# Moving a second gate, a residual and a scaled copy between the engines of a fused Mamba and FFN kernel

## The reference, cut to what matters

```
xbc  = silu(causal conv of 4 taps of the projection)          # X, B, C
Y_intra = (C B^T * decay * dt) X                              # within a chunk
Y_inter = (C H_prev) * exp(cum)      per token and head       # from the chunks before
y = (Y_intra + Y_inter + D_skip * X) * silu(z)                # the gate
out = rmsnorm(y) @ out_proj.T
x = x + layernorm(u + out)                                    # the residual
...
w = silu((h . down_embed) * softmax(top-8 scores))            # per head, 4 heads
x = x + layernorm(w @ up_embed + dense FFN)
```

## Time and profile before

| | |
|---|---|
| median of 3 runs | 2841.09 us (2840.73 to 2841.52) |
| the profiled execution, its own time | 2840.37 us |
| its span, first to last instruction | 2838.7 us |
| mean granted TensorE clock | 0.972 |
| PE busy | 2684.0 us (95%) |
| VectorE busy | 2449.3 us (86%) |
| GpSimd busy | 2100.9 us (74%) |
| ScalarE busy | 1737.2 us (61%) |

### The profile page before, as it was taken

One profiled execution on the slowest core, in us unless ns is written; L12 is line 12 of the kernel. 1 busy time (PEld: TensorE's weight loads), 2 busy tenths in 40 slices (PEclk: granted clock), 3 DMA queues, 4 the chain that ended last, 5 costly groups with the idle time before them and its releaser, 6 DMA issues. The chain is left out here.

```text
span 2838.7 us, 50280 instructions
## 1 busy us (share of the span) xinstructions
PE 2684.0 (95%) x14720; PEld 2215.7 (78%) x14720; DVE 2449.3 (86%) x6310; ACT 1737.2 (61%) x3656; POOL 2100.9 (74%) x2689
## 2 busy tenths in 40 slices
PE   5899999999999999999999999999999999999985
PEld 4778887878887878887878887878887878887864
DVE  4588898998888998889898889988889988989985
ACT  4566666666666566666666666666666666666643
POOL 3377777877777877777877777877777877777866
PEclk9999999999999999999999999999999999999998
DMA  3000000000000000000000000000000000000000
GB/s 133 8 8 12 5 7 11 11 11 11 4 7 11 11 11 11 4 7 11 11 11 11 4 7 11 11 11 11 4 7 11 11 11 8 7 7 11 8 5 8
DMA packets 28182, 34.23 MB, mean 12 GB/s; under 512 B 2672, under 2 KB 27248, under 8 KB 27440
## 3 DMA queue, kind: packets, MB, share of 16 engines
q1 hardware_dynamic: 28144, 33.77, 3.8%
HBM read 25.37 MB, written 8.39 MB: 12 GB/s over the span
## 5 line engine op out<-in xcount | busy, mean ns | idle before, releaser
L1079 DVE SCALAR_TENSOR_TENSOR acc<-bank,cw,acc 128x253 f32<-128x253 f32 (+2 forms) x1920 | 773.5, 470 | 0.0
L1405 PE MATMUL bank<-hT,w_in 128*128 128x256 f32 x2560 | 606.3, 382 | 11.4 <-DVE acc L1079 10.8
L594 POOL TENSOR_TENSOR Em<-ee 128x1024 f32<-128x1024 f32 x256 | 578.8, 2280 | 11.3 <-issue 11.3
L1405 PEld LDWEIGHTS bank<-hT,w_in 128*128 128x128 f32 x2560 | 485.0, 192 | 118.2 <-issue 44.5
L1238 DVE SCALAR_TENSOR_TENSOR Em<-Em,p 128x1024 f32<-128x1024 f32 x256 | 407.1, 1590 | 0.0
L609 POOL TENSOR_TENSOR W<-W,Em 128x1024 f32<-128x1024 f32 x128 | 337.0, 2633 | 8.5 <-ACT Em L887 0.3
L755 ACT ACTIVATE acc<-bank,cb,cw 128x256 f32<-128x256 f32 x640 | 325.1, 561 | 0.0
L1247 DVE TENSOR_TENSOR Em<-Em,products 128x1024 f32<-128x1024 f32 x256 | 310.9, 1214 | 4.5
L887 ACT ACTIVATE Em<-Em,rden 128x1024 f32<-128x1024 f32 x256 | 292.0, 1142 | 33.9 <-DVE Em L1247 33.9
L1574 PE MATMUL products<-w_de,h2T 128*128 128x512 f32 x512 | 234.5, 601 | 17.7 <-DVE Em L1247 17.7
L736 ACT ACTIVATE xbcT<-acc 128x512 f32<-128x512 f32 x320 | 200.6, 627 | 74.1 <-DVE acc L1079 74.0
(11 more groups left out here) (196 smaller groups left out, 5578.9 us busy)
## 6 DMA issues: line engine op xcount, KB each, us to landing
x_in<-x_dram SPq DMA_DIRECT2D x32, 256.0 KB, 2.7
x_res<-x_dram SPq DMA_DIRECT2D x32, 256.0 KB, 2.7
out_dram<-f SPq DMA_DIRECT2D x32, 256.0 KB, 2.2
w_in<-in_wT_dram SPq DMA_DIRECT2D x1, 3080.0 KB, 12.0
w_up<-upT_dram SPq DMA_DIRECT2D x1, 1024.0 KB, 14.7
w_de<-down_eT_dram SPq DMA_DIRECT2D x1, 1024.0 KB, 16.7
w_down<-downT_dram SPq DMA_DIRECT2D x1, 1024.0 KB, 18.7
w_ue<-up_e_dram SPq DMA_DIRECT2D x1, 1024.0 KB, 20.8
```

The source lines that it names most:

```text
L594: nc.gpsimd.tensor_tensor(Em[:, k], bc(ee[:, k, 0:XD], 2, KEYS), bc(ee[:, k, XD:XD + KEYS], 1, XD), ALU.mult).then_inc(E_done.sem, 1)
L1079: ins = V.scalar_tensor_tensor(acc[:, r, a, ahead:], ps[:, a * TOK:(a + 1) * TOK - ahead], cw[:, t, k:k + 1], acc[:, r, a, ahead:], ALU.mu ...
L1405: last = mm(ring[j % 2][:, a * TOK:(a + 1) * TOK], w_in[:, k, at:at + P], hT[:, k, :], start=k == 0, stop=k == DK - 1)
```

## The change

Five edits, all in the order and placement of work; what is computed stays the same.

1. `mixer_state` goes from VectorE to ScalarE. One VectorE multiply of 512 columns becomes eight ScalarE instructions of 64 columns, each with its head's `ecum` as the per-partition scale. It stands after `mixer_B(g, 0)` for c = 0, and after the first expert head for c = 1. ScalarE's `ffn_norm(f)` moves two steps later, behind `mixer_square(g, 1)`.
2. VectorE's `mixer_gate(g, 1)` and `mixer_step(g, 1)` go ahead of `ffn_mask(e, 0, 2)`. On GpSimd, `weigh(e, 1, 0)` now waits for `y_done(g, 1)`, and `mixer_decay(g, 1)` goes ahead of `ffn_root(f)`.
3. `tail_residual(e)` goes ahead of both convolutions 0 and 1. On GpSimd, `tail_root4` follows `tail_root3` at the end of the turn and no longer stands at the start of the next; both stand ahead of `collect(e, 0, 1)` and behind one head of `weigh`.
4. `ffn_last` no longer multiplies by the root and the last product (L1229, twice a group); the reciprocal is multiplied in once for both chunks in `ffn_choose`, and the last product becomes the scale of ScalarE's silu.
5. The matmul of zeros in `ffn_down` goes; the first matmul of the group starts the bank.

```diff
+                if gate is not None:
+                    pool.wait_ge(y_done.sem, y_done.at(gate, CH - 1))
                 for h in heads:
...
                 if a:
                     mixer_dt_abs(g)
-                if b:
-                    tail_root4(e)
...
                     mixer_scale(g, 1)
+                    mixer_decay(g, 1)
                 if c:
                     ffn_root(f)
-                if a:
-                    mixer_decay(g, 1)
-                if b:
-                    weigh(e, 1, 0, 1)
+                if b:
+                    weigh(e, 1, 0, gate=g)
                 if a:
                     mixer_root_y(g)
                 if b:
+                    weigh(e, 1, 1)
+                if a:
+                    tail_root3(g)
+                    tail_root4(g)
+                if b:
                     collect(e, 0, 1)
-                if a:
-                    tail_root3(g)
-                if b:
                     weigh(e, 1, 2, 3)
...
+            def mixer_state(g, c):
+
+                act.wait_ge(Yi_ps.sem, Yi_ps.at(g, c))
+                act.wait_ge(ecum_done.sem, ecum_done.at(g))
+
+                if later(g):
+                    act.wait_ge(yT_ps.sem, yT_ps.at(g - 1, c))
+                    act.wait_ge(sq_done.sem, sq_done.at(g - 1, c))
+                for h in range(HEADS):
+                    last = nc.scalar.activation(yv[:, c, h * HD:(h + 1) * HD], ring[1 - c][:, h * HD:(h + 1) * HD],
+                                                ACT.Identity, scale=ecum[:, 0, c, h:h + 1])
+                last.then_inc(Yi_read.sem, 1)
...
-                    nc.scalar.activation(cls[:], clz[:, c], ACT.Silu, accum_out=clsum[:, c:c + 1])\
+                    nc.scalar.activation(cls[:], clz[:, c], ACT.Silu, scale=last_a[:, 0:1],
+                                         accum_out=clsum[:, c:c + 1])\
...
                     mixer_B(g, 0)
+                    mixer_state(g, 0)
                 if n is not None:
                     mixer_hT(n)
...
                     ffn_experts(e, 0, 0)
                 if a:
+                    mixer_state(g, 1)
                     mixer_yT(g, 0)
-                if c:
-                    ffn_norm(f)
                 if b:
                     ffn_experts(e, 0, 1)
                 if a:
                     mixer_yT(g, 1)
                     mixer_square(g, 1)
+                if c:
+                    ffn_norm(f)
...
+                V.tensor_tensor(masked, masked, bc(rden[:].rearrange("p c h -> p (c h)"), 2, NC), ALU.mult)\
+                    .then_inc(clz_done.sem, 1)
...
-                V.scalar_tensor_tensor(clz[:, c], clz[:, c], last_a[:, 0:1], bc(rden[:, c], 2, NC),
-                                       ALU.mult, ALU.mult).then_inc(clz_done.sem, 1)
+                V.tensor_copy(last_a[:], fA[:, EXPERTS - 1:]).then_inc(last_done.sem, 1)
...
-                conv(0)
                 if b:
                     tail_residual(e)
-                conv(1)
+                conv(0, 1)
...
                 if a:
-                    mixer_state(g, 0)
                     mixer_scores(g, 0)
...
                 if b:
                     ffn_mask(e, 0, 1)
-                if a:
-                    mixer_state(g, 1)
                 if b:
                     ffn_times(e, 0, 1)
-                    ffn_mask(e, 0, 2)
                 if a:
                     mixer_gate(g, 1)
                     mixer_step(g, 1)
                 if b:
+                    ffn_mask(e, 0, 2)
                     ffn_times(e, 0, 2)
...
-                    mm(f0[:], zero_b[:], mask_b[:].rearrange("p h t -> p (h t)"), start=True, stop=False)
                 for i in range(FT):
                     last = mm(f0[:, c * D:(c + 1) * D], hid[:, i, c * P:(c + 1) * P], w_down[:, i, :],
-                              start=False, stop=False)
+                              start=c == 0 and i == 0, stop=False)
```

More of the change, by code:

```diff
@@ L123, in sandwich @@
         ident_b = sb("ident_b", [P, P], BF16)
-        zero_b = sb("zero_b", [P, P], BF16)
         mask_b = sb("mask_b", [P, 4, P], BF16)
@@ L270, in sandwich @@
         Z_done = sig("Z_done", CH * RH)
-        clz_done, cls_done = sig("clz_done", CH), sig("cls_done", CH)
+        clz_done, last_done, cls_done = sig("clz_done"), sig("last_done", CH), sig("cls_done", CH)
         W_part, W_done = sig("W_part", CH * (RH - 1)), sig("W_done", CH)
@@ L341, in _ @@
             nc.gpsimd.memset(mask_b[:], 0.0).then_inc(own_pool, own.one())
-            nc.gpsimd.memset(zero_b[:], 0.0).then_inc(own_pool, own.one())
             nc.gpsimd.memset(halo[:], 0.0).then_inc(own_pool, own.one())
@@ L582, in tail_root4, with weigh @@
                 nc.gpsimd.tensor_tensor(shift4[:], rs4[:], neg_mean4[:], ALU.mult).then_inc(root4.sem, 1)
-            def weigh(e, c, *heads):
+            def weigh(e, c, *heads, gate=None):
+                if gate is not None:
+                    pool.wait_ge(y_done.sem, y_done.at(gate, CH - 1))
                 for h in heads:
@@ L654, in do_group @@
                 if b:
-                    collect(e, 0, 1)
+                    weigh(e, 1, 1)
                 if a:
                     tail_root3(g)
+                    tail_root4(g)
                 if b:
+                    collect(e, 0, 1)
                     weigh(e, 1, 2, 3)
@@ L875, in ffn_experts @@
                 if 0 in heads:
-                    act.wait_ge(clz_done.sem, clz_done.at(e, c))
+                    act.wait_ge(clz_done.sem, clz_done.at(e))
+                    act.wait_ge(last_done.sem, last_done.at(e, c))
                     if c or later(e):
@@ L1096, in mixer_scores @@
                                     Ldec[:, 4 * q:4 * q + 4, :], ALU.mult).then_inc(sL_done.sem, 1)
[L1098 to L1106, removed]
             def mixer_step(g, c):
@@ L1221, in ffn_choose @@
                 V.reciprocal(rden[:].rearrange("p c h -> p (c h)"), den[:]).then_inc(rden_done.sem, 1)
+                dve.wait_ge(rden_done.sem, rden_done.at(e))
+                dve.wait_ge(own_dve, own.n)
+                V.tensor_tensor(masked, masked, bc(rden[:].rearrange("p c h -> p (c h)"), 2, NC), ALU.mult)\
+                    .then_inc(clz_done.sem, 1)
             def ffn_last(e, c):
                 dve.wait_ge(A_ps.sem, A_ps.at(e, c))
-                dve.wait_ge(rden_done.sem, rden_done.at(e))
-                V.tensor_copy(last_a[:], fA[:, EXPERTS - 1:]).then_inc(own_dve, own.one())
-                dve.wait_ge(own_dve, own.n)
-                V.scalar_tensor_tensor(clz[:, c], clz[:, c], last_a[:, 0:1], bc(rden[:, c], 2, NC),
-                                       ALU.mult, ALU.mult).then_inc(clz_done.sem, 1)
+                if c or later(e):
+                    dve.wait_ge(cls_done.sem, cls_done.at(e, c - 1))
+                V.tensor_copy(last_a[:], fA[:, EXPERTS - 1:]).then_inc(last_done.sem, 1)
             def ffn_mask(e, c, *heads):
```

## The result

| | before | after |
|---|---|---|
| median of 4 runs, us | 2841.31 | 2936.72 (2935.62 to 2939.07) |
| ratio | | 1.0337 [1.0319, 1.0355] |
| profiled execution: time, span | 2840.37, 2838.7 | 2936.50, 2934.8 |
| mean granted TensorE clock | 0.972 | 0.959 |

What follows compares the result with a forecast made beforehand. PE (95% busy) was taken to set the pace, losing 3.8 us per turn to a wait for VectorE's gate. Chain +0.9, clock +1.65, zeros -0.2 gave +2.35 per turn, +70 on 2840.4: 2911 us, range 2789 to 2950.

Steps and rivals of the forecast that it cites:

- State on ScalarE, matmul of zeros, last expert's term at no cost or a small gain: Eight ScalarE instructions take 1.75 us, costing nothing; PE's zeros matmul saves 0.2 us per turn; last expert's term 0.
- The gate: Chunk 1's y_done 1.5 us after T, end of PE's intra-chunk product; PE's 2.13 us wait and half clock go.
- Third mask and store behind GpSimd's products, fourth mask clean: VectorE behind the gate: GpSimd's products hold the shared port against third mask (over 2 us) and store; fourth mask 1.27.
- The root's gap: Ahead of the residual, VectorE idles 1.2 us for GpSimd's root, a gap convolution 0 filled before.
- Pair 2: PE's projections needing convolution 0 start at 1384.2, 0.9 us later than before; PE waits up to 4.7 us.
- The clock: PE behind the new wait at pair 2: half clock again, costing the same 1.65 us per turn.
- Sum: Per turn +0.9 chain, +1.65 clock, -0.2 zeros = +2.35 us; over 30 turn boundaries +70 us.
- Behind pair 2, at nothing: Later in the turn, GpSimd's weigh and root come some 3 us later but its waits absorb that: no cost.
- Rival 2: GpSimd's products miss VectorE's masks and store; convolution 0 ends 1381.8: 2840 or 2789; chances 0.08 and 0.14.
- rival 1: VectorE in time everywhere, PE has no long wait: gain 4.0 us per turn, 2721 us; chance 0.08.
- Rival 3: No half clock behind PE's new wait, chain as forecast: +0.7 us per turn, 2861 us; chance 0.12.
- Rival 4: ScalarE's state too slow, PE waits for Yi_read: up to 1.7 us more per turn, 2960 us; chance 0.05.

Runs made afterwards that it cites:

- b3: Kernel before with only mixer_state moved from VectorE to ScalarE, ffn_norm left in its place: 2794.6 us, ratio 0.9835.
- c1: Changed kernel with the moves of the gate and of the residual undone, GpSimd's part included: 2798.9 us, ratio 0.9852.
- c2: Changed kernel with only the gate's move undone, GpSimd's part included; residual still ahead of convolution 0: 2867.5 us, ratio 1.0085.
- a3: Changed kernel with VectorE's third mask ahead of the second gate again, GpSimd's wait for y_done kept: 2925.3 us, ratio 1.0302.
- a2: Changed kernel without GpSimd's wait for y_done ahead of weigh(e, 1, 0): 2932.4 us, ratio 1.0322.
- c4: Kernel before with the gate's move alone, but without GpSimd's wait for y_done: 2859.8 us, ratio 1.0064.
- a4: Changed kernel with 19 unused matmuls of 512 columns between ffn_A and pair 2, filling PE's wait: 2866.3 us, ratio 1.0094.
- b4: Kernel before with only VectorE's tail_residual moved ahead of convolutions 0 and 1, GpSimd's order unchanged: 2878.1 us, ratio 1.0129.
- a1: Changed kernel with VectorE's tail_residual back between convolutions 0 and 1: 2917.0 us, ratio 1.0270.
- b1: a1 with GpSimd's tail roots and collect placed as in the kernel before: 2903.2 us, ratio 1.0220.
- b2: Kernel before with the gate's move alone, GpSimd's wait for y_done included, tail roots left in place: 2907.3 us, ratio 1.0232.
- c3: Kernel before with nine unused matmuls of 512 columns filling PE's wait ahead of the transposes of y: 2797.3 us, ratio 0.9848.

## Why the prediction was right, step by step

- *State on ScalarE, matmul of zeros, last expert's term at no cost or a small gain*: 1.75 us as taken, no wait for `Yi_read`. What I missed is that, alone, the state's move is the best part of the change (b3, -45 us), since it brings the third mask in ahead of GpSimd's decay. I had costed it as cover only. The `ffn_norm` that moved along costs VectorE a wait of 1.1 us (c1, c2, a3), which the prediction did not name; in the changed kernel it is hidden, since the store comes later there anyway.
- *The gate*: forecast `y_done` at T + 1.5, measured 1324.08 + 0.69 = T + 1.52; multiply 0.69; the wait of 2.13 and its half clock gone.
- *Third mask and store behind GpSimd's products, fourth mask clean*: as forecast, 2.08, 2.08 and 1.27. That GpSimd's new wait produces this order was shown by a2 and c4, where the multiply is contended and the third mask is not.
- *The root's gap*: 1.2 taken, 1.51 measured; the residual clean, 0.88.
- *Pair 2*: forecast T + 18.1, measured T + 18.36; forecast wait 4.7, measured 4.73. Each step of the chain from T ends within 0.25 us of its forecast, so the mechanism held and not only the number.
- *The clock*: here the size was off. I took 1.65 us from the earlier trace rows. The two groups behind the wait take 3.78 and 4.24 where 1.89 and 3.62 are full speed, so 2.5 us; a4 took out 70.4 us, 2.35 in each of 30 turns. Half clock was granted from 1340 to 1346, and part of that lay in the wait itself. That it was 2.5 in each settled turn does not make it a fixed price: behind waits of one length c2 and b4 paid different prices from turn to turn.
- *Sum*: 2.35 per turn forecast; with 0.25 more for the chain and 0.85 for the clock it is 3.4, the measured 88.75 - 85.33 (1.15 from T to pair 2, 2.25 from pair 2 to T, as the stretches above show). That accounts for the 26 us between 2911 and 2937 and a little more.
- *Behind pair 2, at nothing*: true of the changed kernel, where PE waits for VectorE nowhere else, but only because PE was late itself; that this term held is in part luck. In a1, with pair 2 3 us earlier, the waits of pairs 6 and 9 took back most of the gain. Their tie to GpSimd's later adds is read from the timelines; b1 moved the roots back and the waits went, but it moved other port waits as well.

Rival 2 (clean port) came nearest in c2, where both masks took 1.27 us and the store 1.27 (0.69 clean): pair 2 came at T + 16.9 in place of the rival's 15.7 and waited 2.74. No run came near rival 1 (all hidden, 2721). Rival 3 (no half clock) is what a4 makes artificially. Rival 4 fell with the 1.75 us of the state.

By parts, on the kernel before: state -45 (b3), gate +68 (b2), and VectorE's part of the residual's move +38 (b4; GpSimd's roots stay in place there). These do not simply add up to the +95 of the whole. With edits 1, 4 and 5 in place (c1) the gate alone costs 104 (2903.2 - 2798.9), the whole of edit 3 alone 69 (2867.5 - 2798.9), and the two together 138 (2936.7 - 2798.9). So the gate's move costs more once the state has moved. A likely reason, not shown by a run of its own: by then PE waits only 0.46 us for the gate, at full clock, so there is little left to win against the same port waits. The two moves together cost less than the sum of both; why was not followed.

The residual's +38 alone can be followed in b4's trace: the mean turn is 1.45 us longer, of which 0.59 is the wait for pair 2, 0.1 lies behind pair 2, and the rest is the longer half clock behind the gate's wait.

The fastest kernel here is b3, 2794.6 us, edit 1 alone: faster than the kernel before and the changed one. The filled kernel before (c3, 2797.3) is as fast within the spread of the runs. Filling b3's remaining waits, or moving its residual away from GpSimd's products, was not tried.

## What to carry to other kernels

Before a wait on the leading engine is removed, walk the chain that this wait was hiding up to the next point where the engine waits for it, and count the waits for a shared port in it: here the 2.1 us gained at the gate were paid back as 4.7 at pair 2. A wait that keeps one engine out of the way of one instruction only shifts its work onto the next ones, so list what the other engine will need the port for just after the release. Undo such a bundle edit by edit: one part of this 3.4% loss was a 1.6% gain.

## What the runs showed of the hardware

- A wait of PE can cost clock on top of its length. Behind the wait of 2.13 us the rows show 1.65 us of it; filling that wait with matmuls that nobody reads made the kernel before 43.5 us faster (31 waits, 1.4 us each), and filling the one of 4.32 made the changed kernel 70.4 us faster.
- The price is not fixed by the length of the wait. In c2 pair 2 waited 2.74 us in each turn, and the turns took 84.9, 87.9 and 86.6 us by how long 0.50 was granted; in b4, behind 2.15 us, the same sixteen matmuls took 6.20 us in one turn and 5.21 in the next. I had expected one price for both waits.
- In these traces a VectorE instruction with two SBUF inputs waits for GpSimd's whole instruction, however short it is itself: one of 64 columns, 0.21 us in the kernel before, took 1.99 us (1187.12 to 1189.11) in a1, where a GpSimd add ran from 1186.68 on, two adds in 4.78 us.
- Eight ScalarE instructions of 64 columns with a scale from memory take 1.75 us, 0.33 each by itself and 0.2 from start to start. The Trainium skill ("ScalarE: Activation LUTs", section "What ACT_TABLE_LOAD costs") gives terms from which an estimate for this form is 2.0; the trace has 1.75 and decides.
